# Inverse roots of the row moments: one GpSimd power operation in place of ScalarE's square root and VectorE's reciprocal

## The reference

```python
def _layernorm(x, axis=-1, eps=1e-05):
    m = jnp.mean(x, axis=axis, keepdims=True)
    v = jnp.var(x, axis=axis, keepdims=True)
    return (x - m) / jnp.sqrt(v + eps)

x = x + _L0_attn_ref(_layernorm(x), ...)    # attention, 16 heads, quantised activations and weights, two more norms inside
x = x + _L0_xattn_ref(_layernorm(x), ctx, ...)      # cross attention with a tanh
x = x + _L0_ffn_ref(_layernorm(x), ...)     # batch norm over all rows, then a memory of product keys
x = x + _L1_attn_ref(_layernorm(x), ...)    # attention
x = x + _L1_xattn_ref(_layernorm(x), ctx, ctx, mask, ...)   # cross attention with tanh-bounded logits
x = x + _L1_ffn_ref(_layernorm(x), ...)     # 8 experts, 4 of them per row
```

## Time and profile before

| | us |
|---|---|
| median of 3 runs | 2658.8 |
| lowest and highest of the 3 | 2653.73, 2671.69 |
| the profiled execution's own time | 2659.77 |
| span of the profiled execution | 2658.0 |
| PE / DVE / ACT / POOL busy | 2379.5 / 2112.2 / 1949.4 / 775.0 |

### The profile page before, as it was taken

The page is one execution under the profiler, slowest core; times in us unless marked ns, Lnnn a source line. Parts: engine busy times, 40 slices in busy tenths (PEclk is TensorE's granted clock), DMA queues, the critical chain, the costliest instruction groups (busy, mean ns, idle before and its releaser), DMA issues.

```text
span 2658.0 us, 95278 instructions
## 1 busy us (share of the span) xinstructions
PE 2379.5 (90%) x35020; PEld 1880.5 (71%) x35020; DVE 2112.2 (79%) x5477; ACT 1949.4 (73%) x3624; POOL 775.0 (29%) x917
## 2 busy tenths in 40 slices
PE   2999963876899999999989999899889999999999
PEld 1666642554788888888857766566868888888887
DVE  6777789687799999999767777688677777777776
ACT  1788863546799999999657777688667777777776
POOL 0455520004466666666433333111030000000000
PEclk9999985876799999999989999899689999999999
DMA  5000000000000000000020000111011111111111
GB/s 181 1 0 0 0 16 0 1 0 2 2 0 0 0 0 0 0 0 0 2 65 0 0 0 0 35 43 43 7 48 53 52 56 52 56 52 56 52 56 44
DMA packets 56803, 64.77 MB, mean 24 GB/s; under 512 B 7696, under 2 KB 35088, under 8 KB 56592
## 3 DMA queue, kind: packets, MB, share of 16 engines
q1 hardware_dynamic: 56720, 63.65, 7.8%
HBM read 59.17 MB, written 4.46 MB: 24 GB/s over the span
## 4 chain that ended last, share of the span: by engine, by line
PE 70%; DVE 16%; issue 10%; DVEq 1%; ACT 1%; POOL 0%; DMA 0%; ACTq 0%; POOLq 0%; SPq 0%
PE ps L957 5%; PE ps L1000 5%; PE ps L985 5%; PE ps L1228 4%; PE ps L1230 4%; PE ps L1206 4%; PE ps L1229 4%; PE ps L1208 4%; PE ps L1207 4%; PE ps L1013 3%; PE ps L972 3%; DVE work L1677 2%; PE ps L1126 2%; DVE work L1678 2%; DVE work L1684 2%
## 5 line engine op out<-in xcount | busy, mean ns | idle before, releaser
L501 POOL TENSOR_TENSOR work<-work,consts_sb 128x1024 f32<-128x1024 f32 x128 | 246.2, 1924 | 442.8 <-ACT work L625 404.1
L1138 PE MATMUL ps<-work 32*32 32x32 f32 x16384 | 250.1, 224 | 46.7 <-DVE work L1632 30.4
L1138 PEld LDWEIGHTS ps<-work 32*32 32x32 f32 x16384 | 242.8, 145 | 61.1 <-issue 61.1
L1812 DVE TENSOR_TENSOR h_low<-consts_sb,h_up 128x1024 fp32r<-128x1024 f32 x128 | 158.4, 1238 | 110.8 <-ACT h_up L849 110.7
L1433 DVE TENSOR_REDUCE work<-ps 128x8 f32<-128x512 f32 x256 | 169.9, 686 | 88.2 <-PE ps L957 82.3
L1206 PE MATMUL ps<-a_low,w_up 128*128 128x512 f32 x512 | 203.0, 397 | 0.9 <-DVE a_low L1787 0.9
L1228 PE MATMUL ps<-h_low,d_up 128*128 128x512 f32 x512 | 199.6, 390 | 2.0 <-DVE h_low L1812 2.0
L1208 PE MATMUL ps<-a_up,w_low 128*128 128x512 f32 x512 | 200.4, 391 | 0.0
L1207 PE MATMUL ps<-a_up,w_up 128*128 128x512 f32 x512 | 200.2, 391 | 0.0
L1812 DVE TENSOR_TENSOR h_low<-small_w,h_up 128x1024 fp32r<-128x1024 f32 x128 | 158.9, 1241 | 51.7 <-ACT h_up L849 51.7
L1230 PE MATMUL ps<-h_up,d_low 128*128 128x512 f32 x512 | 199.3, 389 | 0.0
(11 more groups left out here) (270 smaller groups left out, 6359.7 us busy)
## 6 DMA issues: line engine op xcount, KB each, us to landing
gates_spread<-gate_rows SPq DMA_DIRECT2D x128, 256.0 KB, 3.1
ctxT_all<-in_ctxT SPq DMA_DIRECT2D x1, 4096.0 KB, 12.8
work<-in_ctx SPq DMA_DIRECT2D x64, 64.0 KB, 1.8
work<-in_ctxT SPq DMA_DIRECT2D x64, 64.0 KB, 1.8
out<-x_all SPq DMA_DIRECT2D x16, 256.0 KB, 3.5
big<-in_up SPq DMA_DIRECT2D x1, 2048.0 KB, 8.5
consts_sb<-in_consts SPq DMA_DIRECT2D x1, 936.0 KB
w<-in_key_inT SPq DMA_DIRECT2D x1, 512.0 KB, 3.7
```

Source lines behind the costliest of these rows:

```text
L501: pool.tensor_tensor(KX[:, u].rearrange("p b (h k) -> p b h k", h=PER_SET), KC[:, u].unsqueeze(2).to_broadcast([P, 2, PER_SET, SEQ]), own_ ...
L1138: ins = pe.matmul(psW[rows, n // 16, :, n % 16], XT[rows, T.u, :, n], YT[rows, T.u, :, n], start=True, stop=True)
L1812: dve.tensor_tensor(h_low[:, n], hid[n], h_up[:, n].bitcast(F32), ALU.subtract).then_inc(h_split, 1)
```

## The change

VectorE still adds 1e-5 and raises `var_ready`. GpSimd now waits for `var_ready` and raises row 0 of `t64` to the power of a constant block that holds -0.5, straight into the destination; it raises `std_ready`. VectorE's wait for `std_ready` stands ahead of its next operation. ScalarE's square roots and VectorE's reciprocals and drains at the ten sites are gone.

```diff
+        less_half = sb("less_half", [P, NT])
...
         block.gpsimd
         def _(pool):
+            pool.memset(less_half[:, :], -0.5)
             pool.memset(ones[:, :], 1.0).then_inc(ones_ready, 1)
 
+            def rsqrt(n, dst, width=NT):
+                if n == 1:
+                    pool.wait_ge(ones_ready, 1)
+                pool.wait_ge(var_ready, n)
+                pool.tensor_tensor(dst, t64[:, 0, 0:width], less_half[:, 0:width], ALU.pow).then_inc(std_ready, 1)
...
+            rsqrt(1, rs[:, :])
+            rsqrt(2, t64[:, 6, :])
             pool.wait_ge(phase, PHASE["attn0"])
             staggered(nc, pool, NT, [(0, spread(ATTN["attn0"])), (0, add_output_bias)])
 
+            rsqrt(3, rs[:, :])
+            rsqrt(4, t64[:, 6, :])
+            rsqrt(5, rs[:, :])
+            rsqrt(6, rs[:, :])
+            rsqrt(7, sc[:, 28:29], 1)
             pool.wait_ge(phase, PHASE["memory"])
...
+            rsqrt(8, rs[:, :])
             pool.wait_ge(phase, PHASE["attn1"])
             staggered(nc, pool, NT, [(0, spread(ATTN["attn1"]))])
+            rsqrt(9, rs[:, :])
             pool.wait_ge(phase, PHASE["cross1"])
...
             staggered(nc, pool, NT, [(0, ctx_values)])
+            rsqrt(10, rs[:, :])
...
         block.scalar
-            def deviations(n, width=NT):
-                act.wait_ge(var_ready, n)
-                act.activation(t64[:, 1, 0:width], t64[:, 0, 0:width], ACT.Sqrt).then_inc(std_ready, 1)
...
-            deviations(1)
-            deviations(2)
             act.wait_ge(phase, PHASE["attn0"])
...
-            deviations(9)
             act.wait_ge(phase, PHASE["cross1"])
...
         block.vector
-            def rsqrt(dst, src, width=NT):
+            def rsqrt(src, width=NT):
 
                 seen[0] += 1
                 dve.tensor_scalar(t64[:, 0, 0:width], src, EPS, None, ALU.add).then_inc(var_ready, 1)
                 dve.wait_ge(std_ready, seen[0])
-                dve.reciprocal(dst, t64[:, 1, 0:width])
-                dve.drain()
```

More of the change, by code:

```diff
@@ L673, in _ @@
                                     (3, copy_q("attn0")), (4, copy_v(b0)), (2, copy_k("attn0")), (5, copy_probsT(b0, 0))])
-            deviations(3)
             def squares(T):
@@ L684, in _ @@
             staggered(nc, act, NG, [(0, squares)])
-            deviations(4)
             def copy_ints(T):
@@ L692, in _ @@
             staggered(nc, act, NG, [(1, copy_ints)])
-            deviations(5)
             act.wait_ge(phase, PHASE["cross0"])
@@ L729, in _ @@
             staggered(nc, act, NG, [(1, copy_xnT), (3, copy_pT), (2, x_exps), (1, entangle)])
-            deviations(6)
             def keep_xT(T):
@@ L737, in _ @@
             staggered(nc, act, NG, [(1, keep_xT)])
-            deviations(7, 1)
             act.wait_ge(phase, PHASE["memory"])
@@ L785, in _ @@
             staggered(nc, act, NT, [(0, normed), (2, key_exps), (5, hidden), (2, best_one_hot), (3, below_least), (3, scaled_one_hots)])
-            deviations(8)
             act.wait_ge(phase, PHASE["attn1"])
@@ L810, in _ @@
             staggered(nc, act, NT, [(2, tanhs), (4, copy_oT(OUTT["cross1"])), (2, bounded_exps)])
-            deviations(10)
             act.wait_ge(phase, PHASE["routing"])
@@ L1361, in _ @@
             mean, var = mv[:, 0, :], mv[:, 1, :]
-            rsqrt(rs[:, :], var)
+            rsqrt(var)
             dve.tensor_tensor(t64[:, 5, :], rs[:, :], rs[:, :], ALU.mult)
@@ L1369, in _ @@
             dve.drain()
-            rsqrt(t64[:, 6, :], t64[:, 5, :])
+            rsqrt(t64[:, 5, :])
             dve.tensor_tensor(rs[:, :], rs[:, :], t64[:, 6, :], ALU.mult)
@@ L1603, in _ @@
             dve.drain()
-            rsqrt(sc[:, 28:29], sc[:, 27:28], 1)
+            rsqrt(sc[:, 27:28], 1)
             dve.tensor_tensor(sc[:, 13:14], sc[:, 28:29], K("gamma"), ALU.mult)
```

## The result

The changed kernel takes 2744.4 us (median of 4 runs, 2740.93 to 2747.85), against 2660.66 us for the kernel before (median of 4 runs, 2653.73 to 2671.69). The ratio is 1.0315, with a 95% interval of 1.0297 to 1.0333. Its profiled execution has a span of 2743.8 us, 85.8 us more than before. The change is slower, and its time lies 47 us above the upper end of the range (2697 us).

A forecast was written before the change was run, and what follows sets the result against it. The prediction took the unhidden barriers between stages as what the change touches in a mostly TensorE-bound kernel. Its terms, 9.9 - 1.3 - 0.6 = +8.0 us on 2659.77, gave 2667.8 us, range 2650 to 2697.

The forecast's parts named there:

- What bounds a site: At each wide site nothing hides the wait; addition to next operation goes from 1.15 us to p + 0.45 us.
- The price p: Time of GpSimd's power on 64 columns: 1.8 us, bounded by 0.35 below and 4.9 above.
- 9 x (p - 0.70): Time added at the nine wide sites together: +9.9 us, with bounds of -3.2 and +37.8 us.
- Site 7, put at 0: The one-column site takes 0.66 us from addition to next operation and stays there, with 0.24 us for its power.
- the dear power: Rival: GpSimd's power makes each barrier several us longer; 2695.7 us at 4.9 us a power; chance 0.22.
- the 2 in 10 that were left outside: Chance of a time outside the range, from a power dearer than its bound or table loads worth more.
- The floor: Lower bound for the power: a plain two-input operation on GpSimd, 0.35 us for 64 columns.
- The cheap rival: Rival: the power is nearly as cheap as an addition, 0.35 us; kernel at 2654.7 us, no change; chance 0.17.
- Table loads: Eleven loads of 1.28 us go; two count, -1.3 us ahead of cross1's tanh, -0.6 us ahead of memory's exponential.
- GpSimd against VectorE: Rule against the change: GpSimd is slower elementwise; a power of twice the reciprocal, 1.1 us, adds 3.6 us at nine sites.
- Clock and first call: Possible errors at single sites: a longer first power, or longer gaps keeping TensorE's clock low; no size given.

## Why the prediction was wrong

- **What bounds a site: right.** Nothing hides it. p + 0.45 us was forecast from the addition to the next operation; it is 10.55 + 0.38 at site 1, and between p + 0.31 and p + 0.55 at all wide sites.
- **The price p: wrong, and the step that failed.** I took 1.8 us and bounded it at 4.9; it is 10.55. The bound counted at most 30 elementary steps at 2.45 ns a column. One column costs 158 ns, 65 times 2.45. No run shows of what steps a power on GpSimd is made, nor how many they are: 20 and 30 were guesses, and so was the 1.2 ns for a step. The guess of at most 30 was then used as a bound, although no row limits how much work a power is. Why a column costs 158 ns stays open. The term 9 x (p - 0.70) was put at +9.9 us (bounds -3.2 and +37.8); with the measured p it gives 88.7, and the nine sites show 87.8. Site 7, put at 0, grows by 0.16 us: its power takes 0.55 us and not 0.24.
- **The rival that came true** is the dear power, at 0.22, with its threshold (p from 3.8 us) right and its size cut off by the same bound. The range ended at 2697 us for that reason. A power beyond the bound had a share of the 2 in 10 that were left outside, but no price.
- **The floor: right.** A plain operation of this shape was put at 0.35 us and takes 0.32. The cheap rival's 5.1 us less for the whole kernel lies at the edge of what the multiplication measured, 7.7 less (5 to 11).
- **Table loads: right in place, size not settled.** 1.3 us ahead of cross1's first tanh and 1.3 ahead of memory's first exponential show at the spots. For the kernel all eleven together measured 1 us less, between 4 less and 2 more. The forecast of -1.9 lies in there, and so does no effect. The drain of 1.38 us that the Trainium skill's page "ScalarE: Activation LUTs" (section "What ACT_TABLE_LOAD costs") adds to a load does not show in any of these traces: in the run with the early tanh the load starts 0.01 us behind the root.
- **GpSimd against VectorE.** The Trainium skill's page "GPSIMD Engine Reference" (section "3.1 Elementwise — side-by-side cycle accounting") gives a factor of 1.96 for an addition. From a factor of two I worked out 1.1 us for the power. The direction was right, the size was not: a power takes 33 times the 0.32 us of a multiplication of the same shape on the same engine, so the factor for an addition says nothing about a power.
- **Clock and first call: no part in it.** The first power takes 10.55 us like the last, and TensorE's busy time is 2380.3 us against 2379.5.

## What to carry to other kernels

An operation that no row of the profile shows has no upper price that can be argued from other operations; where it stands on the path several times, measure it alone on an idle engine before building on it, or keep a heavy tail. What counts at a barrier is the length of the chain through it, so ten microseconds on an idle engine are as bad there as on a busy one. If the consumers wait piece by piece, only the first piece can be on the path: in parts, the same power cost 0.3 us at two sites and nothing at four. A change may bundle a good plan with a bad operation: with a multiplication in the power's place, the same plan was 7.7 us faster than the kernel before.

## What the runs showed of the hardware

- A power on GpSimd (two f32 inputs) takes 0.4 us plus 0.158 us a column, for 1 partition as for 128, and regardless of the values tried (64 columns: 10.54 us on one partition, 10.55 in the kernel); a multiplication of 128x64 takes 0.32 us.
- In the changed kernel VectorE's operation behind a power starts 0.03 us after its end at six sites and 0.15 to 0.28 us after it at four; GpSimd starts 0.15 us behind VectorE's addition at the first site and 0.08 us at the other nine.
- A power that starts while VectorE runs L1528 of norm0 takes longer by about the time to the end of VectorE's series: 5.84 us in place of 2.9 for 16 columns, 8.80 in place of 8.0 for 48, 3.97 in place of 1.0 for 4. In the changed kernel, where VectorE waits for the power, the seven powers into `rstd` stay within 10.550 and 10.587 us.
- A table load took 1.28 us every time. Ahead of the roots it started 0.02 us behind the previous activation (1668.03), in ScalarE's wait; ahead of cross1's first tanh it started only behind the scores (1678.21).
